# A 32-group attention and feed-forward pipeline: single-pass products in two blocks, a joined feed-forward product, scores on two row groups, and a later feed-forward stage

## The chip, the cores and the metric

The kernel runs on one core of a Trainium2 chip. The metric is device time in microseconds (us) of one execution; lower is better. Engines are named as in the profile: PE is the matmul engine (TensorE), PEld its weight loads, DVE the vector engine, ACT the scalar engine, POOL GpSimd, SP the queue that starts the DMA transfers.

## The reference, cut to what matters

The input x has 128 sequences of 32 rows and 512 columns. Four layers follow one another:

```python
# 1. a mixing of the 32 rows of each sequence, with weights that depend on the condition
att = softmax(gelu(gelu(cond @ W0 + b0) @ W1 + b1) @ W2 + b2)
y = einsum('boi,bih->boh', einsum('bk,koi->boi', att, weight), x) + (att @ bias_k)[:, :, None]
# 2. attention: 32 query heads, 8 key/value heads, head width 16, rotary positions, causal
out = softmax(mask(rope(y @ Wq) . rope(y @ Wk) / 4)) . (y @ Wv) ; x1 = x + out @ Wo
# 3. a grouped convolution along the 512 columns (9 taps, 4 groups), plus a context bias
z = conv1d(x1, w, groups=4) + ctx[:, :, None] + bias
# 4. feed-forward: a dense product, a router over 15 slots, and 8 low-rank experts
probs = softmax(z @ router_W.T + router_b); w = top-8 probabilities, mapped to experts
o = z @ base_W.T + base_b + 2 * einsum('bter,eor->bto', (z @ A.T) * w, B) ; out = x1 + o
```

## The kernel before

**Tiling.** A group is four sequences, so 128 rows by 512 columns; there are G = 32 groups. Every engine runs the same hand-written software pipeline, `iterate(eng, steps)`: `steps(t)` for t from -1 to 33, and in one call the engine works on several groups of different age. I call one `steps(t)` a period. `live(u)` is true when group u exists, `peeled(t, n)` marks one-off preparations. Engines meet through named semaphores (`y_ps`, `zs_sb` and so on; `_ps` says that a PSUM bank was written, `_sb` that an SBUF tile was).

**Precision.** Large products are made of three single-pass products of fp32r halves (`product`: hi by hi, hi by lo, lo by hi; L375 of the profile, and L516 for `base`, L535 to L537 for `lora`). The hi half is a copy on ACT, the lo half a subtraction on DVE or POOL. The smaller products take fp32 operands, and each is two MATMUL instructions in the trace; a transpose is one.

**Order of a period in the kernel before.** All queues run in program order.
- PE: `qkv(t)` (12 products of 512 columns, 12 of 256), `project(t-1)` (12 of 512), `transpose_qk(t)` (5 transposes, L504, L505), `base(t-2)` (12 of 512, L516), `transpose_hw(t-2)` (L509), `scores(t)` (two bf16 products of 512 columns that put the causal mask into the bank, L526, and four fp32 products of 256 columns, L528), `lora(t-2)` (3 of 512), `conv(t-1)` (12 fp32 products of 128 columns, L545), `transpose_p(t)` (8 transposes, L552), `mix(t+1)` (4 fp32 products, L470), `values(t)` (8 fp32 products of 68 columns, L562), `heads(t-1)` (12 single-pass products of 256 columns with the router and the experts' A, L375 on `ar_hi`), `transpose_o(t)` (4 transposes, L579).
- DVE: `oT_lo`, `route(t-2)`, `rope(t)` with the copies of v (L958 to L967), `route2(t-2)` (L933 to L947, ends with `hw`), `x1(t-1)` (L1016), `keys(t)` (the masked copy kT, 1,024 columns, L974), eight copies of x1 by phase (L282), `hwT_lo`, `softmax(t)` (L983, L985, twice each), the sum for the output (L1042), `zs(t-1)` (L1048), `ys(t+1)` (L1060), `normalize(t)` (L992, L994, twice each).
- ACT: `oT_hi`, the exponential of the router, qT, eight copies of x1 by phase, `hwT_hi`, two exponentials (L723), two copies prT, `z_hi`, `y_hi`, `arS` (the copy of what `heads` made).
- POOL: `z_lo(t-1)`, `y_lo(t+1)`, `x1b(t-1)` = x1 + base_b (L800). SP: loads of x for the mixing (xm) and for the sum (xr), the store of the output.

**What waits for what around the change.** `scores` wait for qT and kT, `transpose_p` for both exponentials, `values` for prT, `heads` for `z_lo`, `transpose_hw` for `hw`, `transpose_o` for the normalized heads, and the next `qkv` comes behind it on PE. DVE's chain from the scores is: softmax, then whatever stands behind it in DVE's program.

## Time and profile before

| | |
|---|---|
| runs of the kernel before | 747.69, 748.32 and 748.35 us; median 748.32 us |
| profiled execution | 748.08 us; its span, first to last instruction, 746.1 us |
| PE busy | 711.7 us, 95% of the span |
| weight loads, DVE, ACT, POOL busy | 628.5, 543.9, 272.5, 147.6 us |
| chain that ended last | PE 82%, ACT 7%, POOL 5%, DVE 3%, issue 2% |
| granted PE clock | 0.99 of full speed over the span |

The page says which engine is busy, the chain says what released the last instruction step by step, and the timeline gives one period in order. The kernel is periodic, so one period of the middle tells nearly all; the first two periods and the two after the last group are read apart.

### The profile page before, as it was taken

The numbers are of one execution on the slowest core, as the hardware profiler recorded it, in microseconds if no ns is written. First come the engines' busy times: TensorE is split into PE (matmuls) and PEld (weight loads), VectorE is DVE, ScalarE is ACT, GpSimd is POOL, SyncE is SP. The second block draws the span as 40 slices with busy tenths as digits, with TensorE's granted clock in tenths as the row PEclk, the third lists the DMA queues.
The fourth block names the chain that finished last, engine by engine and source line by source line (L and its number), as shares of the span: only waits on it lengthen the run. The fifth ranks groups of instructions, "written<-read, shape, count | busy, mean of one in ns | idle before, by whom it ended". The sixth has DMA issues, their size and how long they took to land.

```text
span 746.1 us, 13077 instructions
## 1 busy us (share of the span) xinstructions
PE 711.7 (95%) x4478; PEld 628.5 (84%) x4510; DVE 543.9 (73%) x1424; ACT 272.5 (37%) x635; POOL 147.6 (20%) x116
## 2 busy tenths in 40 slices
PE   5879999999999999999999999999999999999985
PEld 4578888888888888888888888888889888888874
DVE  5457787777778777777877777788777777877763
ACT  4135433333443333344333323433333344333331
POOL 5232201222221122222102222210122222012211
PEclk9979999999999999999999999999999999999999
DMA  7751100111110011111100111110011111001000
GB/s 189 169 242 29 43 17 27 42 42 42 42 42 31 15 38 42 42 42 42 40 16 28 42 42 42 42 42 14 28 42 42 42 42 42 19 23 42 29 29 29
DMA packets 27392, 35.43 MB, mean 47 GB/s; under 512 B 11651, under 2 KB 13347, under 8 KB 26998
## 3 DMA queue, kind: packets, MB, share of 16 engines
q1 hardware_dynamic: 26374, 34.88, 15.1%
q10 hardware_dynamic: 864, 0.14, 0.1%
q0 software_dynamic: 144, 0.28, 0.1%
q8 instruction: 6, 0.10, 0.1%
q14 instruction: 4, 0.03, 0.0%
HBM read 26.36 MB, written 8.93 MB: 47 GB/s over the span
## 4 chain that ended last, share of the span: by engine, by line
PE 82%; ACT 7%; POOL 5%; DVE 3%; issue 2%; DMA 0%; POOLq 0%; SPq 0%; DVEq 0%
PE ps L375 37%; PE ps L516 11%; PE ps L545 11%; PE ps L528 8%; POOL z_lo L786 5%; ACT raw L644 4%; PE ps L552 2%; PE ps L579 2%; ACT z_hi L644 2%; PE ps L504 2%; PE ps L562 1%; PE ps L535 1%; PE ps L536 1%; PE ps L537 1%; PE ps L526 1%
## 5 line engine op out<-in xcount | busy, mean ns | idle before, releaser
L786 POOL TENSOR_TENSOR z_lo<-raw,z_hi 128x512 fp32r<-128x512 f32 x32 | 40.8, 1274 | 561.1 <-ACT z_hi L644 561.1
L545 PEld LDWEIGHTS ps<-convW,x1ph 128*128 128x128 f32 x768 | 90.6, 192 | 2.8
L545 PE MATMUL ps<-convW,x1ph 128*128 128x128 f32 x768 | 90.9, 275 | 0.0
L644 ACT ACTIVATE x1ph<-raw 32x128 f32<-32x128 f32 x256 | 78.9, 308 | 32.0 <-DVE raw L1016 29.4
L375 PE MATMUL ps<-wqkv_hi,y_hi 128*128 128x512 f32 (+1 forms) x256 | 90.5, 353 | 0.0
L375 PE MATMUL ps<-wqkv_hi,y_lo 128*128 128x512 f32 (+1 forms) x256 | 87.4, 341 | 0.0
L375 PE MATMUL ps<-wqkv_lo,y_hi 128*128 128x512 f32 (+1 forms) x256 | 87.3, 341 | 0.0
L644 ACT ACTIVATE qk_t<-ps 128x512 f32<-128x512 f32 x32 | 19.1, 598 | 177.5 <-PE ps L505 177.5
L811 DVE TENSOR_TENSOR oT_lo<-ps,oT_hi 128x512 fp32r<-128x512 f32 x32 | 22.1, 692 | 70.8 <-ACT oT_hi L644 70.8
L528 PE MATMUL ps<-qk_t 128*128 128x256 f32 x256 | 66.7, 383 | 4.4 <-issue 2.8
L723 ACT ACTIVATE raw<-raw 128x512 f32<-128x512 f32 x64 | 40.3, 630 | 76.5 <-DVE raw L985 76.5
L562 PE MATMUL ps<-vm,raw 128*128 128x68 f32 x512 | 61.1, 273 | 0.3 <-ACT raw L644 0.3
L562 PEld LDWEIGHTS ps<-vm,raw 128*128 128x128 f32 x512 | 60.1, 193 | 0.6 <-DVE raw L1048 0.6
L282 DVE COPY x1ph<-raw 32x128 f32<-32x128 f32 x256 | 55.6, 217 | 3.0
L528 PEld LDWEIGHTS ps<-qk_t 128*128 128x128 f32 x256 | 49.3, 193 | 9.2 <-issue 0.3
L958 DVE TENSOR_TENSOR network<-ps,cst 128x512 f32<-128x512 f32 x64 | 31.5, 492 | 33.4 <-PE ps L375 33.0
L375 PEld LDWEIGHTS ps<-wqkv_hi,y_hi 128*128 128x128 f32 x256 | 49.3, 192 | 7.6 <-issue 1.5
L375 PEld LDWEIGHTS ps<-wqkv_lo,y_hi 128*128 128x128 f32 x256 | 49.1, 192 | 6.2
L375 PEld LDWEIGHTS ps<-wqkv_hi,y_lo 128*128 128x128 f32 x256 | 48.9, 191 | 6.2
L516 PE MATMUL ps<-base_hi,z_hi 128*128 128x512 f32 x128 | 53.0, 414 | 0.0
L375 PE MATMUL ps<-wo_hi,oT_hi 128*128 128x512 f32 x128 | 49.8, 389 | 1.6 <-DVE oT_lo L811 1.6
L516 PE MATMUL ps<-base_hi,z_lo 128*128 128x512 f32 x128 | 50.5, 395 | 0.0
(168 smaller groups left out, 1530.1 us busy)
## 6 DMA issues: line engine op xcount, KB each, us to landing
xm<-x SPq DMA_DIRECT2D x32, 256.0 KB, 2.6
xr<-x SPq DMA_DIRECT2D x32, 256.0 KB, 2.8
out<-raw SPq DMA_DIRECT2D x32, 256.0 KB, 2.0
convb<-convb_dram SPq DMA_DIRECT2D x1, 2048.0 KB, 12.2
mixb<-mixb_dram SPq DMA_DIRECT2D x1, 1792.0 KB, 8.7
raw<-L_attn_Wq SPq DMA_DIRECT2D x4, 256.0 KB, 4.0
raw<-L_attn_Wo SPq DMA_DIRECT2D x8, 128.0 KB, 4.5
raw<-L_ffn_base_W SPq DMA_DIRECT2D x1, 1024.0 KB, 5.8
```

The costliest lines, as they stand in the source:

```text
L282: last = copy(x1ph[S * j:S * (j + 1), b, 1:P + 1], x1[S * b:S * (b + 1), j, :])
L375: last = mm(dst, a, b, start=(n == 0), stop=(n == 3 * len(left) - 1))
L504: nc.tensor.transpose(ps[:, 2, g * P:(g + 1) * P], qk[:, g * P:(g + 1) * P], ident)
L516: mm(ps[:, 6, :], a[:, j, :], b[:, j, :], start=(n == 0), stop=False)
L528: last = mm(ps[:, h, (b % 2) * 256:(b % 2) * 256 + 256], qT[:, b, :, :].rearrange("p g q -> p (g q)"), kT[:, b, :, :].rearrange("p k m -> ...
L545: last = mm(zo[:, :, b * S:(b + 1) * S], x1ph[:, b, s:s + P], convW[:, s, :, :], start=(s == 0), stop=(s == SHIFTS - 1))
L562: last = mm(ps[:, 4 + k // 4, (k % 4) * NB * VW:(k % 4 + 1) * NB * VW], prT[:, k, :], vm[:, k, :, :].rearrange("p b c -> p (b c)"), start= ...
L644: return nc.scalar.activation(dst, src, ACT.Copy)
L723: nc.scalar.activation(pr.rearrange("p (k b m) -> p b k m", k=NKV, b=NB)[:, 2 * h:2 * h + 2, :, :], sx.rearrange("p (b k m) -> p b k m", b ...
L786: nc.gpsimd.tensor_tensor(z_lo[:, :, :].rearrange("p j n -> p (j n)"), zs, z_hi[:, :, :].rearrange("p j n -> p (j n)").bitcast(F32), ALU.s ...
L811: return v.tensor_tensor(dst, value, hi.bitcast(F32), ALU.subtract)
L958: v.tensor_tensor(a, src, cst[:, C_COS:C_SIN].unsqueeze(1).broadcast_to([P, h, HD]), ALU.mult)
```

## The change

One more stage is put into the pipeline (t runs to 34), the feed-forward part of a group moves one period later, and each period is reordered.

- PE: `queries(t)`, `keys_values(t)`, `lora(t-3)`, `project(t-1)`, `transpose_qk(t)`, `mix(t+1)`, `scores(t)`, `feed_forward(t-2)`, `transpose_p(t)`, `conv(t-1)` for the first sequence, `values(t)`, `conv` for the other three, `transpose_hw(t-2)`, `transpose_o(t)`.
- `feed_forward` joins `base` and `heads`: for each of 12 pairs of halves one product of 384 columns into bank 6 and one of 272 (128 of base, 144 of router and A, before 256) into bank 7. `lora` is split into 384 columns (bank 6) and 128 (bank 5).
- `scores`: the keys are masked for 4 of 8 key heads at a time (kT has 512 columns, not 1,024); eight fp32 products of 128 columns, four on partitions 0 to 63 into bank 0 and four on partitions 64 to 127 into bank 1, in turn.
- DVE: `zs(t-2)`, `hwT_lo(t-3)`, `oT_lo(t-1)`, rope and v, the sum for the output of t-3 (two operations), `keys(t)`, `x1(t-1)`, `softmax(t)`, the copies by phase, `ys(t+1)`, `route(t-2)`, `last` (the fourth block of base from bank 7 added into x1b), `normalize(t)`, `route2(t-2)`.
- ACT: `hwT_hi(t-3)`, `oT_hi`, `z_hi(t-2)`, qT, copies by phase, exponentials, prT, `arS(t-2)`, `y_hi`, the router's exponential. POOL: `z_lo(t-2)`, `x1b(t-2)` (waits for the sum of t-3), `y_lo`. SP stores group t-3.
- One-off work moves: lora's and half of base's preparation from the first periods into t = 1 and 2.

The core of the diff:

```diff
--- before.py
+++ after.py
...
@@ -32,7 +33,8 @@
 NE = 8
 RANK = 16
 NR = 2 * NE - 1
-NAR = 256
+NAR = 144
+BASE6 = 3 * P
...
@@ -491,6 +498,15 @@
                         [(wqkv_hi[:, c, D:D + 2 * P], wqkv_lo[:, c, D:D + 2 * P]) for c in range(KC)]
                         ).then_inc(qkv_ps, 1)
 
+            def lora(u):
+
+                pe.wait_ge(hwT_hi_sb, u + 1)
+                pe.wait_ge(hwT_lo_sb, u + 1)
+                for n, (a, b) in enumerate(((hwT_hi, lora_hi), (hwT_hi, lora_lo), (hwT_lo, lora_hi))):
+                    mm(ps[:, 6, 0:BASE6], a[:, :], b[:, 0:BASE6], start=False, stop=(n == 2))
+                    last = mm(ps[:, 5, 0:P], a[:, :], b[:, BASE6:D], start=(n == 0), stop=(n == 2))
+                last.then_inc(ffn_ps, 1)
+
...
+                pe.wait_ge(z_hi_sb, u + 1)
+                pe.wait_ge(z_lo_sb, u + 1)
+                wait(pe, out_sb, u)
                 for j in range(PH):
-                    for a, b in ((z_hi, base_hi), (z_hi, base_lo), (z_lo, base_hi)):
-                        mm(ps[:, 6, :], a[:, j, :], b[:, j, :], start=(n == 0), stop=False)
-                        n += 1
+                    for n, (a, b) in enumerate(((z_hi, ffn_hi), (z_hi, ffn_lo), (z_lo, ffn_hi))):
+                        first, final = j == 0 and n == 0, j == PH - 1 and n == 2
+                        mm(ps[:, 6, 0:BASE6], a[:, j, :], b[:, j, 0:BASE6], start=first, stop=False)
+                        last = mm(ps[:, 7, 0:P + NAR], a[:, j, :], b[:, j, BASE6:D + NAR], start=first, stop=final)
+                last.then_inc(ar_ps, 1)
...
@@ -524,27 +540,23 @@
                 for h in range(2):
 
                     mm(ps[:, h, :], ident16[:, :], causal16[:, :], start=True, stop=False)
-                    for b in (2 * h, 2 * h + 1):
-                        last = mm(ps[:, h, (b % 2) * 256:(b % 2) * 256 + 256], qT[:, b, :, :].rearrange("p g q -> p (g q)"),
-                                  kT[:, b, :, :].rearrange("p k m -> p (k m)"), start=False, stop=(b % 2 == 1))
-                    last.then_inc(s_ps, 1)
-
-            def lora(u):
-                pe.wait_ge(hwT_hi_sb, u + 1)
-                pe.wait_ge(hwT_lo_sb, u + 1)
-                mm(ps[:, 6, :], hwT_hi[:, :], lora_hi[:, :], start=False, stop=False)
-                mm(ps[:, 6, :], hwT_hi[:, :], lora_lo[:, :], start=False, stop=False)
-                mm(ps[:, 6, :], hwT_lo[:, :], lora_hi[:, :], start=False, stop=True).then_inc(ffn_ps, 1)
-
-            def conv(u):
+                for b in range(NB):
+                    for h in range(2):
+                        rows = slice(h * P // 2, (h + 1) * P // 2)
+                        last = mm(ps[:, h, b * P:(b + 1) * P], qT[rows, b, :, :].rearrange("p g q -> p (g q)"),
...
+            def conv(u, sequences):
                 pe.wait_ge(ph_act, u + 1)
                 pe.wait_ge(ph_dve, u + 1)
-                zo = ps[:, 5, :].rearrange("p (j t) -> p j t", j=PH)
-                for b in range(NB):
+                zo = ps[:, 1, :].rearrange("p (j t) -> p j t", j=PH)
+                for b in sequences:
                     for s in range(SHIFTS):
                         last = mm(zo[:, :, b * S:(b + 1) * S], x1ph[:, b, s:s + P],
                                   convW[:, s, :, :], start=(s == 0), stop=(s == SHIFTS - 1))
-                last.then_inc(z_ps, 1)
+                return last
 
             def transpose_p(t):
...
@@ -555,7 +567,9 @@
 
             def values(t):
 
-                wait(pe, zs_sb, t)
+                wait(pe, x1_sb, t)
+                if live(t + 1):
+                    pe.wait_ge(ys_sb, t + 2)
                 for k in range(NKV):
...
                     prepare_lora()
-                    prepare_ar()
+                if peeled(t, 3):
+                    pe.wait_ge(lora_lo_sb, 1)
+                if live(t - 3):
+                    lora(t - 3)
                 if peeled(t, 1):
                     pe.wait_ge(wo_hi_sb, NQ)
                     pe.wait_ge(wo_lo_sb, NQ)
                 if live(t - 1):
                     project(t - 1)
+
                 if live(t):
                     transpose_qk(t)
...
                 if peeled(t, 2):
                     pe.wait_ge(mixw_in, 16 * NB)
                 if live(t + 1):
@@ -623,9 +626,27 @@
                 if peeled(t, -1):
                     mixing_weights()
                 if live(t):
+                    scores(t)
+
+                if peeled(t, 2):
+                    pe.wait_ge(lora_lo_sb, 1)
+                if live(t - 2):
+                    feed_forward(t - 2)
+
+                if live(t):
+                    transpose_p(t)
+                if peeled(t, 0):
+                    pe.wait_ge(prep_sb, 1)
+                if live(t - 1):
+                    conv(t - 1, (0,))
+                if live(t):
                     values(t)
                 if live(t - 1):
-                    heads(t - 1)
+                    conv(t - 1, (1, 2, 3)).then_inc(z_ps, 1)
+                if peeled(t, 1):
+                    prepare_base((2, 3))
+                if live(t - 2):
+                    transpose_hw(t - 2)
                 if live(t):
                     transpose_o(t)
...
+                if live(t - 3):
+                    dve.wait_ge(ffn_ps, t - 2)
+                    dve.wait_ge(last_sb, t - 2)
+
+                    wait(dve, out_st, 16 * (t - 3))
+                    out3 = outS.rearrange("p (n j) -> p j n", j=PH)
+                    v.tensor_tensor(out3[:, 0:3, :], ps[:, 6, 0:BASE6].rearrange("p (j n) -> p j n", j=3), x1b[:, 0:3, :], ALU.add)
+                    v.tensor_tensor(out3[:, 3, :], ps[:, 5, 0:P], x1b[:, 3, :], ALU.add).then_inc(out_sb, 1)
+                if live(t):
...
+                    prepare_ar()
+                    prepare_conv()
+                    prepare_experts()
+                if live(t - 2):
+                    route(t - 2)
+                    dve.wait_ge(x1b_sb, t - 1)
+                    v.tensor_tensor(x1b[:, 3, :], ps[:, 7, 0:P], x1b[:, 3, :], ALU.add).then_inc(last_sb, 1)
+                if peeled(t, 0):
 
                     dve.wait_ge(wo_lo_sb, 1)
                 if live(t):
                     normalize(t)
+                if live(t - 2):
+                    route2(t - 2)
 
             iterate(dve, steps)
 
```

## Rows read from the trace of the kernel before

**Rows 1.** Windows view: us; busy of PE, PEld, DVE, ACT, POOL; clock; DMA; GB/s

```profile
308.78:330.41 21.63, 21.44 (x141) 19.11 (x141) 16.47 (x43) 8.04 (x20) 4.01 (x4) 1.00 0.12 36
```

**Rows 2.** Timeline of PE, first part of a period: start us, us, engine, line, operation

```profile
309.10 0.40 PE L375 MATMUL ps<-wqkv_lo,y_hi 128*128 128x512 f32 x1
...
315.78 0.60 PE L504 MATMUL ps<-cst,qk 128*128 128x128 f32 x4
...
316.55 0.39 PE L516 MATMUL ps<-base_lo,z_hi 128*128 128x512 f32 x1
...
319.12 0.27 PE L509 MATMUL ps<-cst,hw 128*128 128x128 f32 x1
...
321.30 0.48 PE L535 MATMUL ps<-lora_hi,hwT_hi 128*128 128x512 f32 x1
...
322.09 2.84 PE L545 MATMUL ps<-convW,x1ph 128*128 128x128 f32 x24
```

**Rows 3.** Timeline of PE, second part of the same period and the next start

```profile
324.76 1.04 PE L552 MATMUL ps<-cst,raw 128*128 128x128 f32 x8
325.64 1.06 PE L470 MATMUL ps<-mixw,xm 128*128 x8
326.53 1.90 PE L562 MATMUL ps<-vm,raw 128*128 128x68 f32 x16
...
328.76 0.28 PE L375 MATMUL ps<-ar_lo,z_hi 128*128 128x256 f32 x1
...
330.05 0.60 PE L579 MATMUL ps<-cst,raw 128*128 128x128 f32 x4
...
330.73 0.39 PE L375 MATMUL ps<-wqkv_lo,y_hi 128*128 128x512 f32 x1
```

**Rows 4.** Timeline of DVE in the same period

```profile
315.16 0.16 DVE L933 TENSOR_REDUCE exZ<-ex 128x1 f32<-128x15 f32 x1
...
316.61 0.35 DVE L947 SCALAR_TENSOR_TENSOR hw<-arS,exR,we 128x128 f32<-128x128 f32 x1
...
317.87 1.22 DVE L974 TENSOR_TENSOR qk_t<-ps,cst 128x1024 f32<-128x1024 f32 x1
319.00 1.83 DVE L282 COPY x1ph<-raw 32x128 f32<-32x128 f32 x8
...
321.07 0.68 DVE L983 TENSOR_REDUCE mx<-ps 128x16 f32<-128x512 f32 x1
...
323.72 1.10 DVE L1042 TENSOR_TENSOR raw<-ps,raw 128x512 f32<-128x512 f32 x1
...
326.85 0.69 DVE L1060 TENSOR_TENSOR ys<-ps,mixb 128x512 f32<-128x512 f32 x1 [1.07 <-PE ps L470]
327.58 0.26 DVE L992 RECIPROCAL rz<-ps 128x16 f32<-128x16 f32 x1
327.87 0.42 DVE L994 TENSOR_TENSOR raw<-ps,rz 128x256 f32<-128x256 f32 x1
```

**Rows 5.** Timeline of ACT in the same period

```profile
322.51 0.63 ACT L723 ACTIVATE raw<-raw 128x512 f32<-128x512 f32 x1 [1.68 <-DVE raw L985]
...
325.40 1.09 ACT L644 ACTIVATE raw<-ps 128x512 f32<-128x512 f32 x2 [0.93 <-PE ps L552]
...
330.25 0.38 ACT L644 ACTIVATE arS<-ps 128x256 f32<-128x256 f32 x1 [2.05 <-PE ps L375]
```

**Rows 6.** Timeline of PE in the prologue, transposes of 128 and 15 rows in turn

```profile
28.49 0.39 PE L449 MATMUL ps<-cst,raw 128*128 128x128 f32 x1
28.81 0.29 PE L450 MATMUL ps<-cst,raw 15*128 15x15 f32 x1
29.03 0.39 PE L449 MATMUL ps<-cst,raw 128*128 128x128 f32 x1
```

**Rows 7.** Timeline of DVE in the first full period (t = 0)

```profile
45.26 0.26 DVE L992 RECIPROCAL rz<-ps 128x16 f32<-128x16 f32 x1 [3.54 <-POOL wo_lo L776]
```

**Rows 8.** Timeline of PE in the tail

```profile
737.12 0.40 PE L516 MATMUL ps<-base_hi,z_hi 128*128 128x512 f32 x1
```

253 lines of the change are left out of this document (114 added, 139 removed).

## The prediction, as put on record before the changed kernel was run

> **What bounds the kernel now.** I read the busy time of single periods first. Periods of the middle are 21.63 us long, at full clock, and PE is busy for 21.44 us of it [rows 1]; DVE has 5 us of air. So PE's queue sets the end, and the timeline of one period gives the price of everything on it. I count from the first query product, 308.87 (the second one, 309.10, less one spacing) [rows 2]. Spacings from start to start:
> - single pass, 512 columns: (319.12 - 316.55) / 11 = 0.234 [rows 2]; 256 columns: (330.05 - 328.76) / 11 = 0.117 [rows 3].
> - fp32, 128 columns, each of its two instructions: (324.76 - 322.09) / 24 = 0.111 [rows 2, 3]. With 68 columns it is the same 0.11: so 0.11 is a floor, not the columns. Transposes take 0.11, mix 8 x 0.11 [rows 3].
> - `scores` with the one transpose before them: 321.30 - 319.12 = 2.18, so 2.07 by themselves plus start, 2.15 by two mask products and eight instructions at 0.215 [rows 2].
>
> PE stands still once: `values` begin at 326.53 and need 16 x 0.11 = 1.74, the second product of `heads` is at 328.76, so the first belongs at 328.64 and PE waited 0.37 us for z_lo [rows 3]. 21.27 us of work and 0.37 of waiting make the period.
>
> **Part one, two blocks.** Four separate single-pass stretches become two. Is a change of precision paid for? Transposes at 330.05 and three more at 0.11 end their slots at 330.49, one 512 product later is 330.72, and the second query product stands at 330.73 [rows 3]. The price of a change is nil, so this gives nothing by itself; what it moves is which waits are covered. z_lo is now made a whole period ahead, so the 0.37 goes.
>
> **Part two, joined product.** 24 products replace 24: 12 x (0.234 + 0.117) = 4.21 before. 384 and 272 columns lie between the rows; on a straight line they take 0.175 and 0.124 (bounds 0.16 to 0.19 and 0.117 to 0.14). 12 x 0.298 = 3.58, so -0.63. Lora goes from 3 x 0.234 = 0.70 to 3 x (0.175 + 0.11) = 0.86, +0.16.
>
> **Part three, tiled scores.** Mask products keep 2 x 0.215. Eight fp32 products become 16 instructions of 128 columns instead of 8 of 256. No row of before shows two row groups at work. Upper bound: they go one after another at the floor, 16 x 0.11 = 1.79, against 1.72 before. Lower bound: the halves overlap. In program order each product has two instructions on one half and then two on the other, so only the second of one half pairs with the first of the other: 9 slots of 0.11, 1.0 us. To either, the change of array shape is added. The prologue has transposes of 128 and 15 rows in turn: a pair takes 0.53 to 0.54 (28.49 to 29.03), 0.32 into the small shape and 0.22 back [rows 6], where 0.11 is the work of the wide transpose; that of the narrow one is not shown apart (bounds 0.05 to 0.11, I take 0.06, as it moves few columns). So 0.21 into it and 0.15 out of it, 0.36 a period (0.31 to 0.38). Scores: 0.43 + 0.36 + 1.0 = 1.8 or 0.43 + 0.36 + 1.79 = 2.6, from 2.15.
>
> I take the overlap: the two halves share no rows, no weights and no bank, the bank split by half is what they need, and the 0.11 floor belongs to a load of weights, which can then run on two row ranges. But it is a choice; nothing in the trace decides it.
> The Trainium skill, "TensorEngine Tiling (Array Packing)", Tiling Modes, says both: different tiles can execute weight loads and products in parallel, and a change of tiling mode drains the engine. The second agrees with the 0.36 of rows 6 and speaks against the change; the first would give the 1.8. The skill's "TensorE: Matmul & The Clock Gate", Part 3, says that weight loads overlap with products only when the row group differs; here the trace disagrees, since loads are busy for 19.11 us beside 21.44 of products in 21.63 [rows 1], nearly all of them on all rows.
>
> **Sum on PE alone:** 21.27 - 0.63 + 0.16 - 0.35 = 20.45 with overlap, 21.3 without. It is not the period, since the new order makes a loop through DVE.
>
> **The loop.** PE: queries, keys and values, projection 6.91 as before [rows 2], lora to 7.77, five transposes to 8.32, mix to 9.21. kT is 512 columns, 0.69 like the other 512-column operations instead of 1.22 [rows 4]; it starts when the last transpose has ended, 8.52, and is ready at 9.21, hidden by mix; scores start at 9.33. DVE's sum for the output (1.10 [rows 4], two operations, I take 1.25, bounds 1.1 to 1.5) is done by 7.5, POOL's x1b (1.54) by 9.1, x1 behind kT by 10.2: all beside PE, with 0.8 spare before softmax. Masks, switch, nine slots: the first bank is ready and softmax starts at 11.07; PE is free for `feed_forward` at 11.13 and leaves it at 14.71.
> DVE from S = 11.07: softmax 323.72 - 321.07 = 2.65; copies by phase 1.86 [rows 4], ready at S + 4.5 = 15.62 with the semaphore; ys ready at S + 5.2 = 16.3. PE: transposes of p need the second exponential, S + 2.77 + 0.63 = 14.47 [rows 5], so `feed_forward` covers it; they end at 15.58; the first sequence's convolution waits 0.04 for the copies and ends at 16.29, which is when ys lets `values` go (16.35). That piece costs nothing, it fills the wait for ys; without it PE would idle 0.7. prT (1.09 for two [rows 5]) is ready at 16.4, when only its first half, ready at 15.95, is needed. Values end at 18.1; their last bank is ready at 18.25. arS (0.38 [rows 5]) stands behind prT on ACT, 16.7, so `route` and `last` run from 16.75 to 17.5, inside the wait for `values`. Normalizing: 0.29 and 0.34 to the next start (0.42 till its own end) [rows 4], after which `route2` starts at 18.92 and lasts 316.61 + 0.35 - 315.16 = 1.80 [rows 4]: hw at 20.72.
> PE has finished the other convolutions at 18.1 + 2.0 = 20.1 and waits 0.7 for hw; `transpose_hw` and `transpose_o` are behind each other, 5 x 0.11; next queries at 21.34. What is late next is thus `route2`, moved from under the projection to the end of the period: PE's wait of 0.37 becomes one of 0.7. Period 21.34 against 21.63, -0.29.
>
> **Ends.** In t = 0 DVE waited 3.54 us for the first wo_lo [rows 7], which follows ys; ys is now ahead of 4 us of preparations, I take -1.9 (0 to -3). t = 1 has half of base's preparation and copies in DVE's loop, +1.0; t = 2 has no lora, -0.7. Tail: the last feed-forward runs by itself; before, 12 products of `heads` end at 737.12 and `base` runs beside the router [rows 8]; now 3.58 stand ahead of the router instead of 1.4, while the start is a little earlier: +0.9 (0 to +3). SP's queue only stores one group later, its transfers have a period of room. Loads for mix(1) must be in before the scores of t = 0; they stand in no chain.
>
> Span: 29 periods x -0.29 = -8.4; -1.6 at the start; +0.9 at the end; -9.1. 746.1 - 9.1 = 737.0, with the 2.0 us around the span of the profiled execution 739.0. That execution (748.08) is 0.2 under the median shown (748.32), so I leave it. By itself this case holds 733 to 744: 0.1 us on the loop is 2.9 us.
>
> **Rivals.**
> 1. The halves don't overlap (slower). The place is the 16 instructions of the tiled scores. For it: the 0.11 floor is as large for 68 columns as for 128, so it looks like serial weight loads [rows 3], and 16 loads at 0.11 stay 16. Softmax starts 0.67 later, `feed_forward` ends at 15.49, the convolution starts behind the transposes of p at 16.37, values, route2 and hw follow: next queries at 22.04, +0.41. 29 x 0.41 - 1.6 + 0.2 + 0.9 = +11.4: 759.5. It decides from about 0.3 us: every 0.11 slot lost above the nine costs up to 3 us, and at 3 lost slots nothing is left of the gain.
> 2. Scores overlap, but the loop eats the gain (no difference): another 0.3 us in softmax to hw, from semaphores between ACT and DVE at arS and the router's exponential that I laid inside other waits. 748.
> 3. The loop through DVE is shorter than laid out, and hw is there when the convolution ends: the period falls by the wait of 0.7 to 20.6; 29 x -1.0: 718. Against it: route2's 1.80 is a chain of its own dependent steps.
> 4. The change doesn't do what it says: as priced, joining the single-pass stretches gives nothing; this is in every case.
>
> **Chances.** Forecast 0.52 (739). Rival 1 0.28 (759.5). Rival 2 0.08 (748). Rival 3 0.05 (718). The rest 0.07: small stalls to either side, 0.03 faster and 0.04 slower. About 0.2% is what a measurement of this kernel can tell from no change. Faster 0.52 + 0.05 + 0.03 = 0.60, same 0.08, slower 0.28 + 0.04 = 0.32. The range reaches from the low end of the forecast's own to rival 1: 733 to 761.
>
> **What the profile will show.** Period from query to query: 21.3, or 22.0. The fp32 products of `scores`: from first start to last start 0.9 us, or 1.7. Their first start 0.3 us after the second mask product's. Softmax's first reduction 11.1 us after the first query. An idle of about 0.7 us on PE ahead of `transpose_hw`, released by hw; none ahead of `feed_forward`. Pairs in `feed_forward` 0.30 us apart. The prediction is wrong if PE waits anywhere else, above all ahead of `values` or of the transposes of p, or if `transpose_hw` doesn't wait.

## The result, and the profile after

| | before | after |
|---|---|---|
| median | 748.01 us (747.67 to 748.35) | 757.80 us (755.91 to 760.62) |
| ratio, 95% interval | | 1.0134 [1.0101, 1.0167] |
| profiled execution, its span | 748.08, 746.1 us | 758.36, 755.1 us |
| period, mean of 20 in the middle | 21.63 us | 21.70 us |

The change makes the kernel slower by 1.3%. I had forecast 739.0 us. Most steps inside a period came out as laid out; the period did not get shorter, and both ends got longer. (Of all executions reported below, one of e_warm's eight ran at a mean granted clock of 0.754 and took 861.3 us; the ratios leave it out.)

Windows view of the changed kernel: one period of the middle, and stretches of t = 1. It answers [rows 1]; columns as there.

```profile
313.58:335.28 21.70, 21.08 (x152) 18.91 (x151) 16.27 (x46) 7.72 (x19) 4.08 (x3) 1.00 0.11 36
...
62.00:64.50 2.50, 1.09 (x8) 0.85 (x8) 2.43 (x9) 1.55 (x3) 0.00 (x0) 1.00 0.00 0
64.50:74.70 10.20, 9.44 (x44) 9.47 (x45) 2.64 (x8) 0.79 (x2) 1.27 (x1) 0.50 0.00 0
```

PE's busy time fell from 21.44 to 21.08 us and the period rose by 0.07: PE now stands still for 0.6 us. The last row is a stretch at half clock, 1.2 GHz, behind 2.5 us in which PE was busy for 1.1.

Timeline of PE in the same period, answering [rows 2, 3]; the last block is the weight loads of the mask products:

```profile
313.81 0.39 PE L377 MATMUL ps<-wqkv_lo,y_hi 128*128 128x512 f32 x1
...
317.76 0.34 PE L506 MATMUL ps<-lora_hi,hwT_hi 128*128 128x384 f32 x1
...
318.56 0.45 PE L377 MATMUL ps<-wo_hi,oT_hi 128*128 128x512 f32 x1
...
321.38 0.60 PE L520 MATMUL ps<-cst,qk 128*128 128x128 f32 x4
...
321.93 1.06 PE L472 MATMUL ps<-mixw,xm 128*128 x8
323.13 0.38 PE L542 MATMUL ps<-causal,ident 128*128 128x512 bf16 x1 [0.15 <-issue]
323.44 1.16 PE L546 MATMUL ps<-qk_t 64*128 64x128 f32 x16
324.53 0.44 PE L531 MATMUL ps<-ffn_hi,z_hi 128*128 128x384 f32 x1
324.81 0.29 PE L532 MATMUL ps<-ffn_hi,z_hi 128*128 128x272 f32 x1
...
328.24 1.04 PE L564 MATMUL ps<-cst,raw 128*128 128x128 f32 x8
329.28 0.91 PE L557 MATMUL ps<-convW,x1ph 128*128 128x128 f32 x6
330.10 2.00 PE L576 MATMUL ps<-vm,raw 128*128 128x68 f32 x16
331.93 2.22 PE L557 MATMUL ps<-convW,x1ph 128*128 128x128 f32 x18
334.62 0.33 PE L584 MATMUL ps<-cst,hw 128*128 128x128 f32 x1 [0.47 <-DVE hw L967]
...
335.55 0.39 PE L377 MATMUL ps<-wqkv_lo,y_hi 128*128 128x512 f32 x1
```

```profile
322.89 0.13 PEld L542 LDWEIGHTS ps<-causal,ident 128*128 128x128 bf16 x2
```

The only idle time of any size is the one ahead of L584, `transpose_hw`: 0.47 us in the record, 0.63 counted from the end of the last convolution's slot (333.88 + 0.11). The record of the first of the two mask products is missing. Both weight loads are there, from 322.89 on, and e_serial, where both products have their records, has them 0.215 apart; so the first one started at 322.91. The first instruction behind a wait lasts longer in its record (0.33 us where the other transpositions have 0.27). Timeline of DVE in the same period, answering [rows 4]:

```profile
322.13 0.69 DVE L996 TENSOR_TENSOR qk_t<-ps,cst 128x512 f32<-128x512 f32 x1 [1.19 <-PE ps L521]
...
324.63 0.69 DVE L1005 TENSOR_REDUCE mx<-ps 128x16 f32<-128x512 f32 x1 [0.84 <-PE ps L546]
...
327.29 1.84 DVE L284 COPY x1ph<-raw 32x128 f32<-32x128 f32 x8
329.16 0.69 DVE L1079 TENSOR_TENSOR ys<-ps,mixb 128x512 f32<-128x512 f32 x1
...
332.76 0.16 DVE L953 TENSOR_REDUCE exZ<-ex 128x1 f32<-128x15 f32 x1
...
334.21 0.35 DVE L967 SCALAR_TENSOR_TENSOR hw<-arS,exR,we 128x128 f32<-128x128 f32 x1
```

I count as in the prediction, from the first query product, 313.81 less a spacing of 0.23, 313.58:

| step | laid out | measured |
|---|---|---|
| transposes of q and k | 7.77 | 7.80 |
| mix | 8.32 | 8.35 |
| mask products (323.13 less 0.215) | 9.33 | 9.34 |
| softmax starts | 11.07 | 11.05 |
| `feed_forward` (324.81 less 0.175) | 11.13 | 11.06 |
| transposes of p | 14.71 | 14.66 |
| first sequence's convolution | 15.62 | 15.70 |
| ys ready (329.16 + 0.69) | 16.3 | 16.27 |
| `values` | 16.35 | 16.52 |
| other convolutions | 18.1 | 18.35 |
| `route2` | 18.92 | 19.18 |
| hw ready | 20.72 | 20.98 |
| next queries (335.55 less 0.23) | 21.34 | 21.73 |

Up to ys the two agree within 0.1 us. Behind ys 0.17 us are lost ahead of `values` and 0.08 ahead of the other convolutions, and 0.13 more between hw and the next queries (0.75 instead of 0.62): 0.39 in this period, 0.36 in the mean of twenty, and the forecast -0.29 became +0.07.

By stretches, with the recorded starts of the queries of t = 2 and t = 31 as the bounds:

| stretch | before | after | difference | laid out |
|---|---|---|---|---|
| to the queries of t = 2 | 70.81 | 75.59 | +4.8 | -0.9 |
| from there to those of t = 31 | 627.4 | 628.5 | +1.1 | -9.1 |
| to the end | 47.92 | 51.03 | +3.1 | +0.9 |

The -0.7 laid out for t = 2 belongs to the middle stretch, and it came: t = 2 took 21.03 us.

### The profile page after: what moved, and what is told of

It reads as the page before. It is cut to its first block, busy times and chain, and to the rows that moved or that the text cites. A ratio compares the mean times of both kernels' runs of the same rounds, so it can differ in the third digit from the quotient of the medians.

```text
span 755.1 us, 13828 instructions
## 1 busy us (share of the span) xinstructions
PE 706.4 (94%) x4830; PEld 630.7 (84%) x4862; DVE 538.0 (71%) x1488; ACT 263.0 (35%) x635; POOL 148.8 (20%) x116
## 3 DMA queue, kind: packets, MB, share of 16 engines
q1 hardware_dynamic: 26374, 34.87, 15.3%
## 4 chain that ended last, share of the span: by engine, by line
PE 81%; DVE 12%; SPq 3%; issue 2%; DMA 1%; ACT 1%; POOL 0%; DVEq 0%
PE ps L377 30%; PE ps L531 10%; PE ps L576 8%; PE ps L532 6%; PE ps L546 5%; PE ps L557 4%; PE ps L472 4%; PE ps L564 4%; PE ps L506 3%; PE ps L590 2%; DVE raw L1016 2%; PE ps L520 2%; PE ps L542 2%; DVE hw L967 2%; PE ps L584 1%
## 5 line engine op out<-in xcount | busy, mean ns | idle before, releaser
L557 PE MATMUL ps<-convW,x1ph 128*128 128x128 f32 x768 | 102.6, 285 | 1.5 <-DVE x1ph L284 1.3
L557 PEld LDWEIGHTS ps<-convW,x1ph 128*128 128x128 f32 x768 | 93.1, 196 | 8.0 <-issue 7.6
L818 POOL TENSOR_TENSOR y_lo<-ys,y_hi 128x512 fp32r<-128x512 f32 x31 | 39.3, 1268 | 278.8 <-ACT y_hi L665 278.8
L814 POOL TENSOR_TENSOR raw<-raw,basebB 128x512 f32<-128x512 f32 x32 | 49.0, 1532 | 138.8 <-DVE raw L1053 138.7
L977 DVE TENSOR_TENSOR network<-ps,cst 128x512 f32<-128x512 f32 x64 | 31.5, 491 | 50.6 <-PE ps L377 49.7
L576 PE MATMUL ps<-vm,raw 128*128 128x68 f32 x512 | 66.8, 286 | 0.0
L1005 DVE TENSOR_REDUCE mx<-ps 128x16 f32<-128x512 f32 x64 | 43.9, 686 | 31.2 <-PE ps L546 31.2
L576 PEld LDWEIGHTS ps<-vm,raw 128*128 128x128 f32 x512 | 62.9, 200 | 3.1 <-issue 0.3
L665 ACT ACTIVATE hwT_hi<-ps 128x128 fp32r<-128x128 f32 x32 | 8.9, 278 | 121.4 <-PE ps L584 121.4
L377 PE MATMUL ps<-wo_lo,oT_hi 128*128 128x512 f32 x128 | 50.4, 394 | 0.0
L377 PE MATMUL ps<-wo_hi,oT_lo 128*128 128x512 f32 x128 | 50.2, 392 | 0.0
```

The source lines that it names most:

```text
L377: last = mm(dst, a, b, start=(n == 0), stop=(n == 3 * len(left) - 1))
L557: last = mm(zo[:, :, b * S:(b + 1) * S], x1ph[:, b, s:s + P], convW[:, s, :, :], start=(s == 0), stop=(s == SHIFTS - 1))
L576: last = mm(ps[:, 4 + k // 4, (k % 4) * NB * VW:(k % 4 + 1) * NB * VW], prT[:, k, :], vm[:, k, :, :].rearrange("p b c -> p (b c)"), start= ...
L665: return nc.scalar.activation(dst, src, ACT.Copy)
L814: nc.gpsimd.tensor_tensor(x1b, x1, basebB[:, :].rearrange("p (n j) -> p j n", j=PH), ALU.add).then_inc(x1b_sb, 1)
L818: nc.gpsimd.tensor_tensor(y_lo[:, :], ys[:, :], y_hi[:, :].bitcast(F32), ALU.subtract).then_inc(y_lo_sb, 1)
```

## Experiments

Where each kernel came out; the period, t = 0, t = 1 and the tail (from the queries of t = 31) are of the one profiled execution. Each ratio compares with executions of the kernel before taken along with that kernel (their medians are 748.0 to 748.7), so it doesn't follow from two medians of this table.

| kernel | median us | ratio to before, 95% | period | t = 0 | t = 1 | tail |
|---|---|---|---|---|---|---|
| before | 748.01 | | 21.63 | 27.29 | 23.39 | 47.92 |
| after | 757.80 | 1.0134 [1.0101, 1.0167] | 21.70 | 26.23 | 29.47 | 51.03 |
| e_hwlate | 737.44 | 0.9841 [0.9814, 0.9867] | 21.02 | 24.08 | 29.00 | 53.11 |
| e_serial | 758.72 | 1.0122 [1.0097, 1.0148] | 21.85 | 23.85 | 28.83 | 50.14 |
| b_tiled | 749.11 | 0.9998 [0.9981, 1.0014] | 21.62 | 27.48 | 22.91 | 50.08 |
| e_warm | 752.37 | 1.0044 [1.0020, 1.0068] | 21.71 | 24.31 | 24.66 | 50.90 |
| e_untiled | 776.22 | 1.0384 [1.0348, 1.0419] | 22.28 | 28.39 | 29.10 | 50.89 |
| e_split | 754.10 | 1.0081 [1.0054, 1.0109] | 21.64 | 25.17 | 29.42 | 50.58 |
| e_values | 752.30 | 1.0047 [1.0027, 1.0067] | 21.57 | 24.73 | 29.55 | 51.08 |
| e_combo | 730.92 | 0.9766 [0.9739, 0.9793] | 20.85 | 24.56 | 25.00 | 55.42 |
| e_csplit | 732.62 | 0.9780 [0.9753, 0.9806] | 20.87 | 27.26 | 24.35 | 54.31 |
| e_cserial | 737.99 | 0.9863 [0.9847, 0.9880] | 21.12 | 23.87 | 24.71 | 54.31 |
| e_ends | 729.31 | 0.9744 [0.9728, 0.9760] | 20.87 | 28.04 | 24.40 | 50.61 |
| e_tail | 728.19 | 0.9737 [0.9712, 0.9763] | 20.87 | 24.22 | 24.78 | 50.68 |
| e_apart | 727.68 | 0.9716 [0.9699, 0.9733] | 20.87 | 26.51 | 24.88 | 51.01 |
| e_beside | 732.86 | 0.9789 [0.9772, 0.9807] | 20.87 | 30.66 | 23.82 | 50.61 |

### The loop through hw

**e_hwlate**, the changed kernel with `transpose_hw` a place later, behind the next queries (ScalarE's and VectorE's splits of it follow it):

```diff
 if live(t):
     queries(t)
+if live(t - 3):
+    transpose_hw(t - 3)
+if live(t):
     keys_values(t)
...
-if live(t - 2):
-    transpose_hw(t - 2)
 if live(t):
     transpose_o(t)
```

> Changed kernel with transpose_hw taken out of the end of the period and put behind the queries of the next one (ACT's and DVE's copies of it moved behind those of the heads). Loop theory: PE waits 0.68 us a period for hw, the last thing of DVE's chain; with it gone the period falls from 21.70 to about 21.05 (the wait less a start), 29 periods give -19 us: 739. Rival, PE or another wait sets the period: the 0.68 turns up ahead of values or of the transposes of p and the period stays above 21.5: 753 or more.

Measured: 737.4 us, period 21.02. Timeline of PE, from the end of a period into the next:

```profile
321.71 2.22 PE L557 MATMUL ps<-convW,x1ph 128*128 128x128 f32 x18
323.77 0.60 PE L590 MATMUL ps<-cst,raw 128*128 128x128 f32 x4
...
327.00 0.27 PE L584 MATMUL ps<-cst,hw 128*128 128x128 f32 x1
```

The transposes of o follow the convolutions 2.06 us on with no idle time, and the transposition of hw sits among the queries. 0.69 us of period are gone for one instruction moved. So PE's wait for hw was the one that set the changed kernel's period, and the 0.26 us that came in behind ys went straight into it (the next run takes 0.13 of them back, and the period falls by as much).

**e_values**, the changed kernel with its waits ahead of `values` changed in two ways: the one for x1_sb dropped (the convolution in front has waited for what follows it), the one for ys put last, behind the one for pT_sb.

```diff
-wait(pe, x1_sb, t)
-if live(t + 1):
-    pe.wait_ge(ys_sb, t + 2)
 for k in range(NKV):
     if k % 4 == 0:
         pe.wait_ge(pT_sb, 2 * t + 1 + k // 4)
+    if k == 0 and live(t + 1):
+        pe.wait_ge(ys_sb, t + 2)
```

> Changed kernel with the wait for x1_sb ahead of values left out (the convolution's wait for the copies by phase, which come after x1, already holds it) and the wait for ys last, on the weight load itself. Restart theory: between ys ready and the first product of values pass 0.24 us, as three waits are worked off one after another on PE's sequencer; with one left it is 0.07 to 0.1; 0.15 less on the loop, 21.55, -4. Rival, the delay is a start of the array after any stop: no change.

Measured: 21.57, 0.135 less, and 752.3 us. In the mean of twenty periods `values` started 0.17 us behind ys instead of 0.25 (I had expected 0.07 to 0.1), its first two instructions are 0.11 apart instead of 0.16, and hw came 0.13 earlier. So it isn't free to have waits that are fulfilled already beside the one that comes last. Which of the two edits brought it, and what the remaining 0.17 us are, no run takes apart.

### The scores

**e_serial**, the changed kernel with the score products of one half ahead of those of the other:

```diff
-for b in range(NB):
-    for h in range(2):
+for h in range(2):
+    for b in range(NB):
         rows = slice(h * P // 2, (h + 1) * P // 2)
```

> Changed kernel with the sixteen instructions of the tiled scores in another order: the eight of the upper half first, then the eight of the lower, so they can't run beside each other. Overlap theory: they take 16 slots of 0.11 in place of 8; the first half's scores are ready when both are now, so softmax starts as now; feed_forward starts 0.85 later, the transposes of p end at 16.4 instead of 15.6 and pass the copies by phase; period +0.5 to +0.6, time +16. Rival, the two halves are only recorded close together and the array works them one after another: no change.

Measured: period 21.85, +0.14, and 758.7 us. PE's and DVE's timeline of e_serial:

```profile
321.78 0.59 PE L542 MATMUL ps<-causal,ident 128*128 128x512 bf16 x2
322.31 1.71 PE L546 MATMUL ps<-qk_t 64*128 64x128 f32 x16
```

```profile
323.50 0.69 DVE L1005 TENSOR_REDUCE mx<-ps 128x16 f32<-128x512 f32 x1 [0.85 <-PE ps L546]
```

The sixteen instructions last 1.71 us instead of 1.16: the halves do overlap in the changed kernel. In the single records of its trace the two instructions of a pair start 0.007 us apart (323.442 and 323.448, 323.655 and 323.662); the second pair starts 0.21 behind the first, the other six 0.11 behind one another, 0.89 from the first start to the last. e_serial isn't free of overlap: the second half's first instruction starts 0.55 us behind the first half's (322.859 and 322.305), while three of the first half are still to come (the records don't name the half, their spacings of 0.21 and then 0.11 do). It took thirteen slots, not the sixteen that I had expected. I had also expected +0.5 of period, and my rival of the prediction had softmax 0.67 later. Neither happens in this order: the first bank is complete after eight instructions, and softmax starts 11.13 us after the recorded first query, as in the changed kernel. Only PE's own part grew, by 0.55, and most of that went into its waits for the copies, ys and hw. So this run prices five of the eight slots that the overlap saves, not rival 1's order, which stays untried. In the whole time it can't be told from the changed kernel (1.0122 and 1.0134, and its t = 0 was shorter).

The Trainium skill, "TensorEngine Tiling (Array Packing)", Tiling Modes, stated both halves of this: tiles work in parallel, and a change of mode drains. The trace agrees with both. Of the drain the rows show: e_serial's mask products start at 321.78 and 0.215 later, and the first 64-row product at 322.31, 0.31 us behind the second one instead of 0.215, so 0.10 on top. The next one follows 0.21 behind that instead of 0.11; if this too belongs to the change of mode, which no run shows, it is the 0.21 us on top that I had in the prediction.

**b_tiled**, the kernel before with the tiled scores and the smaller kT alone. Its edit is that part of the diff shown ahead of the prediction.

> Kernel before with the tiled scores alone (kT of 512 columns, two row groups), nothing else changed. If the tiled scores are worth on PE what the changed kernel shows (1.6 us from the first mask product to the next group, against 2.15): period 21.63 to 21.1, DVE saves 0.53 more on kT, 31 periods: 732. If the exponentials don't make the transposes of p (they now start at the end of both halves, covered by lora and the convolution, 3.4 us, which is what softmax and exp need): 21.3, 738. Rival, row groups cost as much as they save: 748.

Measured: 749.1 us, no difference: the rival's number, and not its cause. PE's timeline of b_tiled:

```profile
318.43 0.27 PE L510 MATMUL ps<-cst,hw 128*128 128x128 f32 x1
...
320.60 0.47 PE L539 MATMUL ps<-lora_hi,hwT_hi 128*128 128x512 f32 x1 [0.38 <-DVE hwT_lo L815]
```

From the transposition of hw to lora it is 2.17 us, as before (319.12 to 321.30 [rows 2]): scores are shorter, and lora waits for the low part of hwT, which VectorE makes behind ScalarE's high part, and that stands behind ScalarE's eight copies of x1 by phase (2.55 us, till 319.83; hwT_hi starts at 319.85). The whole gain turned into a new wait.

**e_untiled**, the opposite: the changed kernel with the scores and the kT of before (1024 columns, four products of 256 columns, two to a bank).

> Changed kernel with the scores of the kernel before (kT of 1,024 columns, four products of 256 columns on all rows, no change of array shape), the rest as changed. Loop theory: kT is ready 0.53 later than now, softmax can start on the first bank before the second is done, so it starts only 0.2 to 0.4 later than now, but feed_forward starts about 1.1 later and pushes the transposes of p and the first convolution out by 0.9; period 21.7 + 0.8 = 22.5, time +24. Rival, the tiled scores bring nothing in this order (as in the kernel before with them alone): 21.7.

Measured: period 22.28, +0.57 where I had expected +0.8, ratio 1.0384 against 1.0134 for the changed kernel, some 19 us. In the mean of twenty periods the transposes of p start 0.98 us later (15.72 against 14.74 from the recorded first query), `values` 0.66 (17.26 against 16.60), hw 0.57. In the new order the tiled scores with the smaller kT carry 0.57 us; in the old one nothing. What an edit is worth depends on what waits behind it.

### The joined base product

**e_split**, the changed kernel with the join undone:

```diff
-mm(ps[:, 6, 0:BASE6], a[:, j, :], b[:, j, 0:BASE6], start=first, stop=False)
-last = mm(ps[:, 7, 0:P + NAR], a[:, j, :], b[:, j, BASE6:D + NAR], start=first, stop=final)
+mm(ps[:, 6, :], a[:, j, :], b[:, j, 0:D], start=first, stop=False)
+last = mm(ps[:, 7, 0:NAR], a[:, j, :], b[:, j, D:D + NAR], start=first, stop=final)
```

with lora in three products of 512 columns and the output in one operation.

> Changed kernel with the join undone: base as 12 products of 512 columns, router and A as 12 of 144, lora as 3 of 512, the fourth block's two extra additions on DVE gone. PE's work is +0.45 in feed_forward and -0.11 in lora. Loop theory: feed_forward runs beside softmax and has 0.16 of air in front of the convolution, values wait for ys; so only 0.1 to 0.2 reaches the period: +3 to +6. Rival, PE's sum sets the period: +0.34, +10.

Measured: period 21.64, 0.065 less, 754.1 us: not slower, but the whole times are hardly apart (the intervals of the ratios overlap), so the 0.065 of the traces is what stands. In the mean of twenty periods `feed_forward` is longer by 0.46, lora and the projection behind it are shorter by 0.13; softmax starts at 11.00 instead of 11.13, and ys is ready at 16.21 instead of 16.35. `values` start no earlier (16.61 and 16.60), since the first half of prT is now later than ys (16.29), but their first two instructions are 0.06 apart instead of 0.16, and hw comes 0.09 earlier. What the join saves falls into time in which PE would wait in front of the convolution and `values`.

### Two repairs and the clock

**e_warm**, the changed kernel with 14 products of no use in t = 1, whose results nothing reads:

```diff
+if peeled(t, 1):
+    for n in range(14):
+        mm(ps[:, 3, :], wo_hi[:, n % 4, 0:P], wo_hi[:, n % 4, :], start=True, stop=True)
 if live(t):
     transpose_p(t)
```

> Changed kernel with 14 single-pass products of 512 columns more, of no use, in the period t = 1 only, between the scores and the transposes of p, where PE stands idle for 3.49 us and where the granted clock falls to half soon after (64.5 to 74.7 us). Clock theory: the idle of t = 1, which feed_forward will fill from t = 2 on, costs the clock; with the filler the clock stays full and t = 1 takes about 24.5 us instead of 29.5: 753. Rival: the products only add their time or nothing, and the clock falls as before: 758 or more.

Measured: 752.4 us, t = 1 in 24.66 us instead of 29.47. The timeline of PE in t = 1, first after, then e_warm:

```profile
62.89 1.09 PE L564 MATMUL ps<-cst,raw 128*128 128x128 f32 x8 [3.49 <-ACT raw L744]
65.26 1.62 PE L557 MATMUL ps<-convW,x1ph 128*128 128x128 f32 x6 [1.28 <-DVE x1ph L284]
66.68 3.52 PE L576 MATMUL ps<-vm,raw 128*128 128x68 f32 x16
69.99 4.15 PE L557 MATMUL ps<-convW,x1ph 128*128 128x128 f32 x18
```

```profile
57.63 2.91 PE L638 MATMUL ps<-wo_hi 128*128 128x512 f32 x12
...
63.74 1.91 PE L576 MATMUL ps<-vm,raw 128*128 128x68 f32 x16
65.49 2.22 PE L557 MATMUL ps<-convW,x1ph 128*128 128x128 f32 x18
```

(Of the 14 products the trace has 12.) `values` took 3.52 us at half clock and 1.91 at full clock, the convolutions 4.15 and 2.22. t = 1 has no `feed_forward` to stand between the scores and the transposes of p, so PE stood still for 3.49 us till 62.89 and for 1.28 till 65.26, and from 64.5 on the clock was at half, for 10.2 us. Products that compute nothing bring 4.8 of the 6.1 us back. The other kernels bear it out: in the six in the new order without these products, the changed one among them, t = 1 takes 28.8 to 29.6 us, in the eight with them 23.8 to 25.0.

**e_combo**, e_hwlate, e_warm and e_values together:

> transpose_hw behind the queries, the 14 filler products in t = 1, and the waits ahead of values as in the run on them alone. If the three act apart: 737.4 - 5 - 1 to 4 (with hw off the loop PE's own sum is close to the period, 20.9 of work): 729. If PE's sum is the bound already: 732.

Measured: 730.9 us, 2.3% faster than the kernel before. Period 20.85. The time lies between the two that I had set against each other (729 and 732), and decides nothing; the next two ask again.

**e_csplit** and **e_cserial**, e_combo with the edits of e_split and of e_serial. Each asks whether PE alone now sets the period.

> The kernel of e_combo with the joined base product undone: base(t-2) as twelve products of 512 columns into bank 6, router and A as twelve of 144 into bank 7, lora as three of 512, the output in one operation (the edit of e_split). Behind the changed kernel this edit lengthened feed_forward by 0.37 us and shortened lora by 0.08, and the period still fell by 0.065, as TensorE waited for other engines there. Theory: in e_combo's order those waits are gone and TensorE's own work sets the period, so that the split costs its 0.29 us: 21.13 us a period, 739 us. Rival: another engine's chain sets e_combo's period too, and the split stays within 0.05 us of 20.85: 731 us (729 to 733).

> The kernel of e_combo with the score products in the order h outer, b inner (the edit of e_serial): the 16 products of 64 rows no longer run two at a time. Behind the changed kernel they then took 0.56 us more, and the period grew by 0.14. Theory (TensorE's own work sets e_combo's period): 0.5 us a period more, 21.35 us, 745.5 us. Rival (still covered by a wait on VectorE): 0.14 us a period as before, 735 us.

Measured: 20.87 and 21.12 us a period. PE's timelines of e_combo, e_csplit and e_cserial, in this order:

```profile
313.15 1.03 PE L564 MATMUL ps<-cst,raw 128*128 128x128 f32 x8
...
316.71 2.22 PE L557 MATMUL ps<-convW,x1ph 128*128 128x128 f32 x18
```

```profile
315.85 1.04 PE L563 MATMUL ps<-cst,raw 128*128 128x128 f32 x8
...
319.12 2.22 PE L556 MATMUL ps<-convW,x1ph 128*128 128x128 f32 x18
```

```profile
315.60 1.03 PE L564 MATMUL ps<-cst,raw 128*128 128x128 f32 x8
...
318.88 2.22 PE L557 MATMUL ps<-convW,x1ph 128*128 128x128 f32 x18
```

From the transposes of p to the last convolutions e_combo takes 316.71 - 313.15 = 3.56 us, the other two 3.27 and 3.28: without the wait for the copies and the restarts behind it this stretch is 0.28 us shorter. That is all the air PE has in e_combo. e_cserial's 0.55 us of scores therefore cost 0.55 - 0.28 = 0.27 of period, and the split costs, in the mean of twenty periods, 0.46 in `feed_forward` less 0.16 in lora and the projection less 0.28, 0.02. Both were measured so (+0.27, +0.03), and both of my theories, which took the air for nil, missed; for e_csplit the rival's number holds, though not its cause, for e_cserial neither does. The join brings 0.03 us a period, in the best order found; in the whole time e_combo and e_csplit can't be told apart.

### The tail, and t = 0

**e_ends**, e_combo with useless products in t = 0 (14 ahead of the transposes of p, 7 ahead of those of o) and behind t = 31; **e_tail**, with the latter alone:

```diff
+if peeled(t, G + 2):
+    for n in range(12):
+        mm(ps[:, 0, :], wo_hi[:, n % 4, 0:P], wo_hi[:, n % 4, 0:D], start=True, stop=True)
 if live(t - 3):
     transpose_hw(t - 3)
...
+if peeled(t, G) or peeled(t, G + 1):
+    for n in range(6):
+        mm(ps[:, 0, :], wo_hi[:, n % 4, 0:P], wo_hi[:, n % 4, 0:D], start=True, stop=True)
 if live(t - 3):
     lora(t - 3)
```

and five more ahead of `feed_forward` in t = 33.

> The kernel of e_combo (730.9 us) with more filler products, whose results nothing reads: 14 ahead of the P transposes and 7 ahead of the o transposes of t = 0 (wqkv_hi by wqkv_hi, bank 3), six ahead of lora in t = 32 and 33, five ahead of feed_forward in t = 33, twelve ahead of transpose_hw in t = 34 (wo_hi by wo_hi, bank 0). In e_combo TensorE idled 3.49 us and 1.89 us in t = 0 and 1.52, 1.55, 1.25 and 3.15 us in the last periods, and the granted clock stood at half from 35.5 to 49.1, 697.7 to 701.1, 711.4 to 718.2 and 721.6 to 731 us. My theory (the half clock behind such idling is what the start and the tail cost): no half clock in these stretches; t = 0 falls from 24.56 to 23 us, and the tail from its 55.42 us by half of the 3.3 us of products at half clock in the first stretch (1.65), half of some 5.2 in the second (2.6), and little in the third, where VectorE's chain runs: to 51.5. Median 731 - 1.5 - 4 = 725.5 us. Rival (the fillers run past the waits and hold up what follows, or the end is VectorE's chain alone): 730 to 733 us. The middle period stays at 20.85 us in both.

> The kernel of e_combo with the filler products of e_ends behind t = 31 alone (six ahead of lora in t = 32 and 33, five ahead of feed_forward in t = 33, twelve ahead of transpose_hw in t = 34), none in t = 0. In e_ends the stretch from the last queries to the end fell from 55.42 to 50.61 us, the 4 us that the half clock was priced at, while t = 0 took 28.04 us instead of 24.56. Theory (the tail's loss is the clock's, and what moved t = 0 has nothing to do with the tail): tail 50.6 us, period 20.85, t = 0 anywhere between 23.9 and 28.4 us, where the kernels with the same t = 0 have it; median 730.9 - 4.8 = 726 us. Rival (the tail's gain in e_ends was luck of one profiled execution): 731 us.

Measured: 729.3 and 728.2 us. The tail fell from 55.42 to 50.61 and 50.68 us in the two, as expected. Windows of the tail, e_combo and then e_tail:

```profile
673.48:728.90 55.42, 42.27 (x249) 37.35 (x248) 29.34 (x92) 13.16 (x36) 8.47 (x6) 0.84 0.07 24
```

```profile
673.57:724.20 50.63, 44.29 (x279) 38.10 (x276) 29.39 (x92) 13.18 (x36) 8.46 (x6) 0.97 0.08 27
```

The mean clock rose from 0.84 to 0.97 of full. The medians moved less than the profiled executions: by the ratios e_tail gains 0.0029 on e_combo, 2 us, with intervals that overlap. In e_ends t = 0 rose to 28.04 us against my expectation of 23, and the median is 4 us above the 725.5 expected. DVE's timelines of t = 0, e_combo and then e_ends, show why:

```profile
37.35 1.80 DVE L915 COPY convW<-cvT 32x32 f32<-32x32 f32 x12
39.16 0.18 DVE L925 CAST emapF<-emapB 128x15 f32<-128x15 int32 x1
```

```profile
37.02 4.28 DVE L930 COPY convW<-cvT 32x32 f32<-32x32 f32 x12
41.31 1.45 DVE L940 CAST emapF<-emapB 128x15 f32<-128x15 int32 x1
```

GpSimd's y_lo starts at 39.54 in the first, behind the copies, and at 38.39 in the second, among them. It was so in all fourteen traces up to there: in three (e_untiled, e_csplit, e_ends) y_lo began within 1.4 us of the first copy, and there it is 15.3 us from the first reduction of softmax in t = 0 to the next queries; in the nine others in the new order it is 11.6, 11.60 to 11.63.

**e_apart** and **e_beside** settle it: e_tail with GpSimd held back until VectorE has made these tables, and e_tail with VectorE held back until GpSimd starts.

```diff
 if live(t + 1) and not peeled(t, -1):
+    if peeled(t, 0):
+        pool.wait_ge(emapF_sb, 3)
     pool.wait_ge(y_hi_sb, t + 2)
```

```diff
 dve.wait_ge(cv_sb, 1)
 dve.wait_ge(pads_sb, 1)
+dve.wait_ge(y_hi_sb, 2)
```

> The kernel of e_tail (728.2 us), with GpSimd's y_lo of t = 0 held back until VectorE has made the convolution's weights and the expert table (convW, emapF, selE, expert). In the traces so far GpSimd began y_lo between 37.7 and 42.5 us. Where that was behind VectorE's twelve small copies into convW, these took 1.8 us and the three small operations behind them 0.18, 0.28 and 0.2 to 1.2; where y_lo began within 1.4 us of the first copy (e_untiled, e_csplit, e_ends), the copies took 4.2 us and the three operations 1.45, 1.55 and 1.42, and t = 0 took 28.4, 27.3 and 28.0 us instead of 23.9 to 26.2. Theory (a small VectorE operation beside a running GpSimd operation waits for it): the copies always take 1.8 us and the expert table's last operation 0.22 instead of 1.2; t = 0 takes 23.9 to 25.5 us (y_lo itself starts up to 1 us later and o's normalisation in t = 0 waits for the first wo_lo behind it); median 728.2 or up to 2 us less. Rival (the slow copies have another cause, transfers of the loads for one): they show up at 4.2 us here too in such an execution, and the wait brings nothing.

> The opposite edit: the kernel of e_tail with VectorE's copies into convW held back in t = 0 until ScalarE has written y_hi, the moment from which GpSimd's y_lo (1.28 us) and then its four wo_lo products (1.5 us each) run. Theory of e_apart: the copies and the expert table now run beside GpSimd by construction, so they take 4.2 us instead of 1.8 and 1.45, 1.55, 1.42 instead of 0.18, 0.28 and 1.2; with the start 2 us later, t = 0 takes 29.5 to 31 us, and the median is 733 to 735. Rival (another cause): the copies take 1.8 us, t = 0 some 26 us, median 730.

Measured: 727.7 and 732.9 us. DVE's timeline of e_apart, then DVE's and POOL's of e_beside:

```profile
38.75 1.81 DVE L926 COPY convW<-cvT 32x32 f32<-32x32 f32 x12
...
41.10 0.22 DVE L941 TENSOR_SCALAR expert<-selE 128x120 f32<-128x120 f32 x1
```

```profile
39.46 8.18 DVE L925 COPY convW<-cvT 32x32 f32<-32x32 f32 x12 [2.28 <-ACT y_hi L677]
```

```profile
40.65 6.01 POOL L808 TENSOR_TENSOR wo_lo<-raw,wo_hi 128x512 fp32r<-128x512 f32 x4
```

Beside GpSimd the twelve copies took 8.18 us, twice what I had expected, and they outlasted it; the three operations of the expert table, which I had expected at 1.45, 1.55 and 1.42 us, then ran behind GpSimd's last one and took 0.18, 0.28 and 0.22. In the single records of the trace GpSimd's five operations, y_lo and the four wo_lo, end at 40.69, 42.24, 43.71, 45.18 and 46.65, and five of the copies end at 40.73, 42.32, 43.76, 45.26 and 46.72, each 0.04 to 0.08 us behind one of them; one more slipped in between two, and the six behind the last one take 0.2 each. Apart, the twelve took 1.81 and the expert table's last operation 0.22 instead of 1.2. So the cause is GpSimd at work at the same time. For t = 0 as a whole e_apart was off: 26.51 us where I said 23.9 to 25.5. From softmax's first reduction to the next queries it took 12.07 us, 0.45 more than the others, the price of the wait; the rest lies ahead of that, where softmax started at 34.29 instead of 32.58 in e_tail. The same is seen in the changed kernel itself, 34.52. In both it is the granted clock (the next section, under the start), not the edit. The whole times of e_apart and e_tail can't be told apart.

## Why the prediction was wrong

The measured 757.8 us lie inside the stated range of 733 to 761, but only because its upper end was rival 1's 759.5. That is luck: rival 1's mechanism was not there, and the time was lost elsewhere. The forecast had the direction wrong.

**What held.** The overlap of the two halves, chosen at 0.52 to 0.28, was right, and so was its size (0.89 us from the first start to the last, for 0.9). So were the spacings of the joined products (0.30 a pair: twelve between 324.64 and the transposes of p at 328.24), lora (317.76 to 318.56, 0.80 for 0.86), kT at 0.69, the order of the whole loop, and that PE would wait for hw, 0.63 us for 0.7. That joining the single-pass stretches gives nothing by itself was read on the rows of before; no run tries it.

**The period.** The step that failed is the loop behind ys: "which is when ys lets `values` go (16.35)". I gave 0.05 us to that release, and it took 0.25 (330.10 behind 329.16 + 0.69), of which e_values shows 0.08 to hang on the waits in front of `values`; `values` themselves (1.83 for 1.75, their first two instructions 0.16 apart) and the way from hw through two groups of transposes to the queries add 0.08 and 0.13. In size this is near rival 2, another 0.3 us between softmax and hw, given 0.08; in place it isn't: rival 2 looked for it between ACT and DVE, and there everything came as laid out (other convolutions to `route2` 0.83 for 0.82, `route2` 1.80 for 1.80). For the middle its "no difference" is about right: 29 x 0.07 = 2 us, less the 0.9 by which t = 2 and t = 3 are shorter than the others, are the 1.1 measured. The prediction said itself that 0.1 us on the loop is 2.9 us, and yet gave this release 0.05.

**The start.** "t = 1 has half of base's preparation and copies in DVE's loop, +1.0": it was +6.1. I had moved `feed_forward` between the scores and the transposes of p, used it as cover in the middle, and did not ask what t = 1 does, which has none. Without it PE stands still for 4.8 us in two pieces, the clock goes to half, and `values` and the convolutions behind it run at 1.2 GHz. e_warm shows the clock's part, 4.8 us; the remainder, 1.3, stands against the 1.0 that I had priced, and what it is made of was not looked at. In t = 0 the gain I expected ahead of wo_lo came (13.4 us from softmax's first reduction to the next queries before, 11.6 after: -1.8 for -1.9), but "loads for mix(1) ... stand in no chain" did not hold: `mix` now stands ahead of the scores, and PE waited 0.72 us for its weights. PE's timeline of t = 0, `mix` of the changed kernel and then of e_tail, and the windows view of the changed kernel right behind:

```profile
30.20 1.96 PE L472 MATMUL ps<-mixw,xm 128*128 128x128 f32 x8 [0.72 <-DMA mixw<-mixw_dram]
```

```profile
29.87 1.11 PE L472 MATMUL ps<-mixw,xm 128*128 128x128 f32 x8
```

```profile
30.40:33.80 3.40, 3.18 (x17) 2.50 (x19) 0.00 (x0) 0.31 (x2) 0.00 (x0) 0.50 0.88 293
```

Softmax began at 34.52 instead of 34.02 before, though its scores are shorter. In eleven of the other thirteen kernels in this order it began between 31.9 and 33.1. The wait by itself doesn't explain it: `mix` starts at 30.20, and at 29.2 to 30.8 in the others. But from there to softmax it is 4.32 us in the changed kernel and 4.31 in e_apart, and 2.71 in eleven of the others (2.80 in e_untiled): in those two alone the clock is at half in between (30.4 to 33.8, and 30.2 to 33.6), and these two are the ones in which PE had stood still longest ahead of `mix` (0.72 and 0.61 us; 0.27 at most elsewhere). So 1.6 us of the changed kernel's t = 0 are the clock's. (The kernel before had half clock from 31.0 to 34.4 itself.) The other kernels with the same t = 0 and full clock there took 23.9 to 25.2 us for it, where VectorE's copies were not held up, instead of 26.2.

**The tail.** +0.9 (0 to +3) was laid out, +3.1 measured. Windows of the changed kernel:

```profile
740.30:743.70 3.40, 3.12 (x11) 3.15 (x12) 0.14 (x1) 0.00 (x0) 1.58 (x1) 0.50 0.21 77
```

At half clock 3.12 us of products lose 1.6 us; that leaves 1.5 for what I had priced at 0.9. For the tail of the changed kernel this is read off the row and not tried; e_tail shows it for e_combo's. It is an upper bound: e_serial and e_split, with full clock in that place but half clock from an earlier point at the very end, have tails of 50.1 and 50.6 us. Nor is the kernel before's 47.92 its only value. b_tiled has the same three waits of PE in its tail (1.57, 1.57 and 2.94 us), but half clock from 734.0 to 740.9 where the kernel before had full clock, and a tail of 50.08. And of seventeen later executions of the kernel before, nine took 747.3 to 748.5 us at a mean clock of 0.989 or 0.990, eight 750.3 to 751.0 at 0.986. So 2 us or more of clock come and go without any edit; that in those executions they lie in the tail is not shown.

**Sum.** 10.2 us of the miss are the middle, 5.7 the start, 2.2 the tail: 18.1, the span of 755.1 less the 737.0 laid out. Only the first was among the rivals, by its size. The stretches outside the loop were priced by their work, not by what PE does while it waits.
